# Router weights laid and split beside W_dt and multiplied in two packed passes, with a buffer of its own for the last feed-forward group's down weights

## The reference

```python
shared = jnp.einsum('ti,hi->th', jax.nn.silu(x @ sh_gate_w.T) * (x @ sh_up_w.T), sh_down_w)
logits = x @ router_weight.T
probs = jax.nn.softmax(logits.astype(jnp.float32), axis=-1)
top_v, top_i = jax.lax.top_k(probs, TOP_K)
...
out = out + jax.nn.sigmoid(x @ shared_gate_w.T) * shared
```

## Time and profile before

| | us |
|---|---|
| median of 3 runs | 2045.21 (2043.68 to 2047.81) |
| profiled execution | 2038.54 |
| its span | 2036.6 |
| PE busy | 1954.8 (96%) |
| DVE busy | 1480.0 (73%) |
| ACT busy | 1197.9 (59%) |
| POOL busy | 798.1 (39%) |

### The profile page before, as it was taken

How to read it: one execution, slowest core, us unless ns; L and a number is a source line. 1 busy time by engine, 2 the same in 40 slices (tenths; PEclk the granted TensorE clock), 3 DMA queues, 4 the chain that set the end, 5 groups by cost and what they waited for, 6 DMA issues and landing times. The chain is left out here.

```text
span 2036.6 us, 32134 instructions
## 1 busy us (share of the span) xinstructions
PE 1954.8 (96%) x10142; PEld 1657.0 (81%) x10142; DVE 1480.0 (73%) x3410; ACT 1197.9 (59%) x2978; POOL 798.1 (39%) x1200
## 2 busy tenths in 40 slices
PE   7999999989999999999999999969999999999996
PEld 5677777768888888888888888858788888888875
DVE  7788565787777777777777778956387778774665
ACT  6752222467666666666666667754376677674342
POOL 4342000685655555555555557942500000001452
PEclk9999999999999999999999999979999999999998
DMA  7343010227000000000000000233799899884563
GB/s 266 124 140 139 16 47 21 84 68 238 22 11 22 11 22 12 9 25 1 22 12 22 32 1 17 61 105 130 257 334 319 310 328 317 310 308 143 198 204 110
DMA packets 82662, 245.28 MB, mean 120 GB/s; under 512 B 10800, under 2 KB 11440, under 8 KB 80592
## 3 DMA queue, kind: packets, MB, share of 16 engines
q1 hardware_dynamic: 77376, 226.46, 32.5%
q0 software_dynamic: 5120, 16.78, 2.3%
HBM read 207.81 MB, written 45.61 MB: 124 GB/s over the span
## 5 line engine op out<-in xcount | busy, mean ns | idle before, releaser
L307 PE MATMUL l_xp<-att_w_hi,xT_hi 128*128 128x512 f32 x512 | 209.8, 410 | 4.8 <-ACT att_qkv L2414 4.3
L307 PE MATMUL l_xp<-att_w_hi,xT_lo 128*128 128x512 f32 x512 | 202.5, 396 | 0.0
L307 PE MATMUL l_xp<-att_w_lo,xT_hi 128*128 128x512 f32 x512 | 202.3, 395 | 0.0
L2443 ACT ACTIVATE att_pr<-att_pr,rec_nb,rec_r 128x384 f32<-128x384 f32 (+2 forms) x256 | 168.6, 662 | 36.3 <-DVE rec_nb L1585 35.6
L946 POOL TENSOR_SCALAR att_pr<-att_pr,rec_ri 128x384 f32<-128x384 f32 (+2 forms) x256 | 140.4, 560 | 124.8 <-DVE rec_ri L1614 121.1
L3874 POOL DMA_INDIRECT y<-moe_rows,moe_slotA x16 | 16.4, 1026 | 414.7 <-DMA moe_rows<-moe_lo_f 411.6
L950 POOL TENSOR_TENSOR att_rot<-att_rot,att_rot 128x384 f32<-128x384 f32 x128 | 129.7, 1014 | 108.9 <-DVE att_rot L1608 108.9
L1581 DVE CUSTOM_DVE_ANT_0 att_pr<-l_dd,att_mask 128x384 f32<-128x384 f32 (+2 forms) x256 | 119.0, 501 | 70.5 <-PE l_dd L307 64.1
L2414 ACT ACTIVATE att_qkv<-l_xp 128x512 f32<-128x512 f32 x128 | 76.3, 596 | 124.9 <-PE l_xp L307 116.4
L1619 DVE TENSOR_TENSOR att_pT_lo<-l_out,att_pT_hi 128x768 fp32r<-128x768 f32 (+2 forms) x128 | 108.7, 849 | 28.9 <-ACT att_pT_hi L2436 28.8
L2436 ACT ACTIVATE att_pT_hi<-l_out 128x768 fp32r<-128x768 f32 (+2 forms) x128 | 92.5, 723 | 41.8 <-PE l_t L307 21.2
(11 more groups left out here) (325 smaller groups left out, 6541.3 us busy)
## 6 DMA issues: line engine op xcount, KB each, us to landing
y<-in_moe_rt SPq DMA_DIRECT2D x59, 704.0 KB, 6.3
y<-in_moe_rt SPq DMA_DIRECT2D x39, 768.0 KB, 6.2
moe_sraw_gu<-in_moe_sgu SPq DMA_DIRECT2D x44, 512.0 KB
moe_sraw_d<-in_moe_sd SPq DMA_DIRECT2D x44, 256.0 KB
moe_xs<-in_zeros SPq DMA_DIRECT2D x39, 256.0 KB, 8.1
moe_lo_f<-moe_xs SPq DMA_DIRECT2D x39, 256.0 KB, 6.5
moe_rows<-moe_lo_f SPq DMA_DIRECT2D x39, 256.0 KB, 6.4
att_raw_w<-in_qkv_w SPq DMA_DIRECT2D x8, 1024.0 KB
```

Of the source, the lines that this page charges most:

```text
L307: mm = pe.matmul(out, lhsT, rhs, start=(i == 0), stop=(i == len(terms) - 1))
L2443: act.activation(p, p, ACT.Exp, scale=r[:, j % 4, g:g + 1], bias=nb_[:, j % 2, g:g + 1], accum_out=sm[:, j % 2, g:g + 1]).then_inc(sa("exp ...
```

## The change

- `W_dt` is laid out with the router's and the shared gate's rows behind its 32 rows, still padded to 128, and is split as before. `keep_router` on POOL copies the ten columns of the high part and of the low part side by side into `keep["rw"]`, 20 columns for each of the 4 chunks, ahead of `scales`. The products of W_in with W_dt overwrite only the first 32 columns.
- The experts phase has no router load and no router split. PE multiplies the 20 packed columns with `xT_hi` and with `xT_lo`: 32 passes. Twenty rows are copied, turned (20x20) and copied again, and a new VectorE addition makes `lg` from the two halves.
- The last group's down weights get a buffer of their own, `wd_last` at 100 KB, over what were raw gate and up weights. The three `tern_d` calls move to the head of VectorE's list for the last group; two other calls swap.
- `qkv` and `raw_o` of the attention swap addresses, and the waits of `first_o` and `first_qkv` follow.

```diff
+        self.wd_last = at("wd_last", [P, CPG, D], F32R)
...
+    def wd(self, g):
+
+        return self.wd_last if g == self.groups - 1 else self.wd_hi
...
+            def keep_router():
+                pool.wait_ge(s("wdt_lo"), 1)
+                for part, w in ((0, wdt_hi), (1, wdt_lo)):
+                    pool.tensor_copy(keep["rw"][:, :, NL * part:NL * (part + 1)], w[:, :, HEADS:HEADS + NL].bitcast(F32))
...
             post.x_add(pool, 1, (3,), True)
+            keep_router()
             scales()
...
             dve.wait_ge(sa("tab"), 4)
+            f.tern_d(dve, FL, CPG, 3 * f.start(FL) + 2 * CPG, (0,))
+            f.tern_d(dve, FL, CPG, 3 * f.start(FL) + 2 * CPG, (1,))
+            f.tern_d(dve, FL, CPG, 3 * f.start(FL) + 2 * CPG, (2,))
             f.split_lo(dve, FL - 1, NB - 1, CPG - 1)
             f.times_up(dve, FL, 0, 0)
             f.times_up(dve, FL, 0, 1)
@@ -1647,14 +1662,11 @@
             f.add_up(dve, FL - 1, NB - 1, False, (1,))
             f.add_up(dve, FL - 1, NB - 1, False, (2,))
             f.add_up(dve, FL - 1, NB - 1, False, (3,))
-            f.tern_d(dve, FL, CPG, 3 * f.start(FL) + 2 * CPG, (0,))
             f.split_lo(dve, FL, 0, 0)
-            f.tern_d(dve, FL, CPG, 3 * f.start(FL) + 2 * CPG, (1,))
             f.times_up(dve, FL, 0, 2)
             f.split_lo(dve, FL, 0, 1)
-            f.tern_d(dve, FL, CPG, 3 * f.start(FL) + 2 * CPG, (2,))
+            f.times_up(dve, FL, 1, 0)
             f.split_lo(dve, FL, 0, 2)
-            f.times_up(dve, FL, 1, 0)
             f.times_up(dve, FL, 1, 1)
...
             def first_o():
-                act.wait_ge(s("w_split"), FFN1_CHUNKS)
+                act.wait_ge(s("down"), NT * f.groups)
                 split_o(0)
 
             def first_qkv():
-                act.wait_ge(s("w_split"), FFN1_CHUNKS)
+                act.wait_ge(s("down"), NT * FL)
                 qkv_out(0, 0)
...
-            sp.dma_start(rw[:], io["router"]).then_inc(s("rw"), 16)
...
             def route_compare():
+                dve.wait_ge(s("lgp"), 1)
+                dve.tensor_tensor(lg[:], lgp[:, :, 0:NL], lgp[:, :, NL:2 * NL], ALU.add).then_inc(s("lg"), 1)
                 dve.wait_ge(s("lg"), 1)
...
-            dve.wait_ge(s("rw_hi"), 1)
-            dve.tensor_tensor(rw_lo[:], rw[:], rw_hi[:].bitcast(F32), ALU.subtract).then_inc(s("rw_lo"), 1)
...
-            act.wait_ge(s("rw"), 16)
-            act.activation(rw_hi[:], rw[:], ACT.Copy).then_inc(s("rw_hi"), 1)
...
-            pe.wait_ge(s("rw_lo"), 1)
             for b in range(NB):
                 bb = slice(BLK * b, BLK * (b + 1))
-                passes(pe, acc[b][:], [(l[:, c, :], r[:, c, bb]) for c in range(KD) for l, r in
-                                       ((rw_hi, xT_hi), (rw_hi, xT_lo), (rw_lo, xT_hi))]).then_inc(s("ps_lg"), 1)
+                passes(pe, acc[b][0:2 * NL, :], [(rw_hl[:, c, :], r[:, c, bb]) for c in range(KD) for r in (xT_hi, xT_lo)]).then_inc(s("ps_lg"), 1)
```

More of the change, by code:

```diff
@@ L535 @@
 HEADS = 32
+NL = 10
 POST_SEMS = ("y_stat", "y_rstd", "y_shift", "y_normed", "x_new", "x_stat", "x_rstd", "x_normed", "turned", "xT_hi",
@@ L600, in mixers_phase @@
         att_place = {"q_hi": 0, "q_lo": 2, "rot": 4, "pr": 8, "mask": 14, "pT_hi": 16, "pT_lo": 19, "o_lo": 22, "v_lo": 26,
-                     "e_hi": 30, "e_lo": 32, "raw_o": 34, "gain": 38, "rot2": 38, "sq0": 15.5, "sq1": 39.5, "sq2": 7, "tab0": 40, "tab1": 44,
+                     "e_hi": 30, "e_lo": 32, "qkv": 34, "gain": 38, "rot2": 38, "sq0": 15.5, "sq1": 39.5, "sq2": 7, "tab0": 40, "tab1": 44,
                      "raw_w": 48, "w_hi": 56, "w_lo": 64, "k_hi": 72, "k_lo": 76, "v_hi": 80, "tab2": 84, "tab3": 88,
-                     "x": 92, "qkv": 100, "o_hi": 104}
+                     "x": 92, "raw_o": 100, "o_hi": 104}
         sa = lambda n: s("att_" + n)
@@ L3719, in experts_phase @@
         gt, eq = sb("gt", [P, NT, EXPERTS, EXPERTS]), sb("eq", [P, NT, EXPERTS, EXPERTS])
-        rw, rw_hi, rw_lo = sb("rw", [P, KD, P]), sb("rw_hi", [P, KD, P], F32R), sb("rw_lo", [P, KD, P], F32R)
+        rw_hl = keep["rw"]
+        lgp = sb("lgp", [P, NT, 2 * NL])
         lg, ex, rank = sb("lg", [P, NT, NL]), sb("ex", [P, NT, EXPERTS]), sb("rank", [P, NT, EXPERTS])
@@ L4219, in _ @@
                         act.wait_ge(s("lg_turned"), 1)
-                        act.activation(lg[:].rearrange("p t e -> p (t e)"), ps_t[:, 0:NT * NL], ACT.Copy) \
-                            .then_inc(s("lg"), 1)
+                        act.activation(lgp[:].rearrange("p t e -> p (t e)"), ps_t[:, 0:2 * NT * NL], ACT.Copy) \
+                            .then_inc(s("lgp"), 1)
                     hs_split(n)
@@ L4338, in _ @@
                         for t in range(NT):
-                            mm = pe.transpose(ps_t[:, NL * t:NL * (t + 1)], lgT[0:NL, P * t:P * (t + 1)],
-                                              ident[0:NL, 0:NL])
+                            mm = pe.transpose(ps_t[:, 2 * NL * t:2 * NL * (t + 1)], lgT[0:2 * NL, P * t:P * (t + 1)],
+                                              ident[0:2 * NL, 0:2 * NL])
                         mm.then_inc(s("lg_turned"), 1)
@@ L4362 @@
 XT_HI, XT_LO, Y_AT, ABS_AT = 512, 512 + 4 * KD * TOK, 512 + 8 * KD * TOK, 512 + 8 * KD * TOK + 4 * NT * D
-KEEP_END = ABS_AT + 160
+KEEP_END = ABS_AT + 480
 def build(nc, io):
@@ L4377, in build @@
             "y": at("y", [P, NT, D], Y_AT),
+            "rw": at("rw", [P, KD, 2 * NL], ABS_AT + 160, F32R),
             "abs_sum": at("abs_sum", [P, 3, FFN1_CHUNKS], ABS_AT),
@@ L4405, in lay_out @@
     rt_d = np.stack([pad_rows(w.T, DK * P).reshape(DK, P, D).transpose(1, 0, 2).reshape(P, DK * D) for w in down])
-    router = pad_rows(np.concatenate([f["L1_ffn_router_weight"], f["L1_ffn_shared_gate_w"]]), P)
+    with_dt = np.concatenate([f["L0_attn_W_dt"], f["L1_ffn_router_weight"], f["L1_ffn_shared_gate_w"]])
     q, kv = f["L1_attn_q_kernel"], f["L1_attn_kv_kernel"]
@@ L4431, in lay_out @@
         "W_out": kxm(f["L0_attn_W_out"]).reshape(P, KD * D),
-        "W_dt": kxm(pad_rows(f["L0_attn_W_dt"], P)), "b_dt": f["L0_attn_b_dt"].reshape(HEADS, 1),
+        "W_dt": kxm(pad_rows(with_dt, P)), "b_dt": f["L0_attn_b_dt"].reshape(HEADS, 1),
         "log_A": c_(f["L0_attn_log_A"].reshape(KD, P).T), "sel": sel, "ident": np.eye(P, dtype=np.float32),
@@ L4437, in lay_out @@
         "moe_sgu": gate_up(f["L1_ffn_sh_gate_w"], f["L1_ffn_sh_up_w"]),
-        "moe_sd": c_(f["L1_ffn_sh_down_w"].T).reshape(SH_CHUNKS, P, D), "router": kxm(router),
+        "moe_sd": c_(f["L1_ffn_sh_down_w"].T).reshape(SH_CHUNKS, P, D),
         "moe_rt": c_(np.concatenate([rt_gu, rt_d], 2)), "route_c": counts, "zeros": np.zeros((P, D), np.float32),
```

9 lines of the change are left out of this document (4 added, 5 removed).

## The result

| | before | after |
|---|---|---|
| median in the first comparison, 4 runs each | 2046.05 us (2043.68 to 2047.81) | 2024.45 us (2022.66 to 2027.71) |
| ratio, 95% interval | | 0.9897 (0.9879 to 0.9915) |
| profiled execution, its span | 2038.54, 2036.6 | 2022.66, 2020.8 |
| whole change again, two other comparisons | 2041.68 and 2042.22 | 2024.78 and 2023.94 |
| ratios of these | | 0.9920 (0.9906 to 0.9935), 0.9910 (0.9886 to 0.9933) |

The forecast was 2040.5 with a range down to 2032.5: the direction was right, the size nearly four times too small. Against the two larger comparisons the change gives 17 to 18 us, against the profiled execution of before 15.8.

The account below looks back on a forecast made before the run. TensorE (PE), busy 96% of the span, was taken as the bound. Terms 2.8 + 2.4 - 0.4 = 4.8, say 4.7 us, off the median 2045.21 gave 2040.5; range 2032.5 to 2043.5.

Parts of the forecast that it names:

- Step 1: Last feed-forward group: PE's stall shortens by 1.3 us and the clock's fall goes, 1.5 more; together 2.8 us gained.
- Step 2: Two POOL copies ahead of the scales: 0.3 us each, fitting in POOL's idle time; zero cost.
- Step 3: Border of the phases: router load, split and subtraction go, PE starts with POOL at 1358.15; shared weights not late.
- rival B: Border: PE does not start with POOL, first pass at 1360.9, 2.75 us lost, total 2043.3; 0.09 together with Rival C.
- Step 4: Router passes at the border: all 32 at the lower clock, 13.7 us; shared products effectively 2.4 us earlier.
- Rival A: Border: the clock rises during the narrow passes after 4.9 us, passes take 9.7 us, total 2034.7; chance 0.36.
- Step 5: After the router passes: larger ScalarE copy and new VectorE addition, nearly no slack; 0.4 us lost.
- Rival C: Last feed-forward group: the stall still drops the clock, 1.5 us less gain, total 2042.0; 0.09 together with rival B.
- E: Whole kernel: removed stalls come back a product later, all 4.7 us gone, about 2045; chance 0.04.
- D: After the router passes: clock stays low through the shared products, slower, 2049.3 after 20 us more; chance 0.04.

Follow-up runs that it names:

- the shift alone: Kernel before with only KEEP_END raised by 320 bytes, moving the buffers of both phases against xT and y: 2036.21 us, ratio 0.9975.
- the feed-forward half: Kernel before with wd_last, VectorE's new order and swapped qkv and raw_o, router unchanged: 2042.66 us (1.0009), again 2040.87 (0.9989).

## Why the prediction was wrong, point by point

**Baseline.** I took the gain off 2045.21, a median of three. In five comparisons with 7 to 28 runs the kernel before has 2041.0 to 2042.2. The absolute forecast was 3 to 4 us too high for this alone; the gain was too small by some 12.

**Step 1, last group: right, and partly given back.** PE loses 0.77 at 336.96 (forecast 0.85), resumes at 352.34 (352.7) after 2.39 us (2.3), the clock stays at 1.00. From 330 to 365 after gains 2.8 us on before, as forecast. The step that failed is "the clock stayed at 1.00 throughout" at the stall of 2.15 us, from which I concluded that such a stall leaves it up. That was one execution: of eleven profiles with the old order it is the only one with 1.00 from 369 to 380, the others have 0.84 to 0.97. With the new order the clock is 1.00 from 350 to 360 in seven of nine profiles (with the old 0.66 to 0.83), and 0.84 from 369 to 380 in seven. So what the change removes in most executions is the first fall. By traces the group's worth is 1.4 net (330 to 400) against a profile that was favourable there, 3.1 to 3.5 against the six with the good distance and the old order (they drift by +1.7 to +2.1), and about 3 by the comparisons with a good distance.

**Step 2: right.** The two copies take 0.41 and 0.21 us at 119.44 and 119.80, and from 110 to 165 after's drift even falls, from +0.6 to +0.3.

**Step 3: right.** PE starts 0.04 us behind POOL's memset; rival B is out. The shared weights' low part starts at 1356.95, before PE's products at 1360.81.

**Step 4: wrong, the largest miss of a term.** I had the spacing right (0.43 and 0.23) and the level wrong. The sentence that failed is "passes on 20 columns are in this nearer to the transposes than to full passes". The stretch 1350 to 1355 that I read it from the earlier trace rows has 3.66 us busy of 5, with gaps, at the attention's end; the narrow passes come back to back. Rival A had it, with 9.7 us; it took 8.6, because the rise came sooner: 2.5 us after the first pass. (In before it came 5.2 us after, not 4.9.) The border gave 9.3 us (7.4 - 3.1 of waiting, 13.6 - 8.6 of passes). The Trainium skill, page "TensorE: Matmul & The Clock Gate", Part 1, goes by how busy PE is, without a word on columns. The seven traces with 20 columns agree with it as far as the rise goes (0.43 to 0.23 us apart within 2.5 to 5.5 us), and I should have let it weigh more than an argument from transposes with gaps.

**Step 5: right.** The addition takes 0.32, the `s_mul` that PE wants comes later; 0.5 us are lost from 1380 to 1410.

**The term that was missing: 320 bytes.** I read `KEEP_END` in the diff as bookkeeping. It moves every buffer of the kernel but xT and y, and I wrote no term for it, not even with a bound. It is worth 4 to 5 us: each of the attention's 1536 projection passes takes 4 to 5 ns less at the new distance. More is gained in the attention (5.4) than stays. Near its end PE stands for 2.1 to 2.2 us before `l_out`, for as long with either distance; within 1 us of that stall's end the clock falls in all twelve profiles with the good distance (0.91 to 0.96 in 1290 to 1330, one line above), and in two of the eight others (at 1333 and 1334). From 1300 to 1345 1.5 us go in after, 2.7 with the shift alone. Why the clock falls more often there with the good distance no run shows.

**Sum.** Distance 4.7, border 9.3, last group 3, -0.5 behind it and 1.5 at the first gather: 18.0, against 16.9 and 18.3 measured. The terms come from different comparisons, and that of the last group is the least certain, so the agreement is no proof of each. In place of the forecast's 4.7 stood 2.8 for the group, 2.4 for the border and nothing for the distance. Rival C happened in two of the nine profiles with the new order (0.83 from 350 to 360), not in after's; E and D did not happen.

## What to carry to other kernels

A constant that moves buffers is an edit of its own: give it a term, and when a kernel changes everywhere by a fraction of a per cent, compare the spacing of one kind of instruction before looking for a wait. Where PE streams many products whose two operands lie in separately laid-out regions, try a few distances between the regions; it costs one number, and here it was worth half of what the removed wait and passes brought. Don't read from one profile whether a stall of 2 us drops the clock.

## What the runs showed of the hardware

- The spacing of fp32 passes of 512 columns depends on the distance between the stationary and the moving operand in memory: 226 to 229 ns when it is a multiple of 256 bytes, 233 to 234 at 32, 64, 96, 128, 160, 192 and 224 bytes more (the feed-forward's gate and up products at 192: 230). It showed with xT as either operand, and in both phases. Why it is so, no run shows.
- Passes with 20 stationary columns take as long as those with 128 at either clock level (0.43 us, and 0.23 within 2 ns), and the clock rises under them, in seven of seven traces.
- After a stall of the same length the clock sometimes falls and sometimes not, in the same kernel: the feed-forward half's two traces have stalls of 2.39 and 2.15 us, one with 1.00 behind both, the other with a fall behind each.
